# Turning seven of the sixteen Wk tiles on VectorE, and interleaving the context's second half with Wk's first tile

## The reference, cut to what matters

```python
Q = einsum('btx,dx->btd', layernorm(x), Wq) + bq
K = einsum('bpx,dx->bpd', ctx, Wk) + bk            # ctx: 4 x 64 x 2048, Wk: 2048 x 2048
attn = softmax(einsum('btd,bpd->btp', Q, K) / sqrt(2048))
x = x + tanh(g_xattn) * einsum('btp,bpd->btd', attn, ctx)
x = x + tanh(g_ffn) * ffn(layernorm(x))            # router, top-8 slots, uncertainty gate
```

## Time and profile before

| | |
|---|---|
| median of 3 runs | 1095.2 us (1094.51 to 1099.56) |
| the profiled execution | 1094.26 us |
| its span in the profile | 1092.5 us |
| TensorE busy | 1053.9 us, 96% of the span |
| VectorE, ScalarE, GpSimd busy | 70%, 51%, 17% |
| keys stage | from 0 to 137.2 us of the span |

### The profile page before, as it was taken

One profiled execution on the slowest core, in us unless ns is written; L12 is line 12 of the kernel. 1 busy time (PEld: TensorE's weight loads), 2 busy tenths in 40 slices (PEclk: granted clock), 3 DMA queues, 4 the chain that ended last, 5 costly groups with the idle time before them and its releaser, 6 DMA issues. The chain is left out here.

```text
span 1092.5 us, 19631 instructions
## 1 busy us (share of the span) xinstructions
PE 1053.9 (96%) x6890; PEld 1009.0 (92%) x6890; DVE 768.6 (70%) x1844; ACT 552.8 (51%) x860; POOL 182.7 (17%) x351
## 2 busy tenths in 40 slices
PE   6999999999998999999999999999999994999997
PEld 6999999998998999999999999999999994888886
DVE  6655546456746877777777778776877766788785
ACT  3333477654625454545454545454554543555643
POOL 0610000000002222222223131312222322000000
PEclk9999999999999999999999999999999996999999
DMA  7433646689449982744343744437353517999999
GB/s 280 145 134 135 236 175 253 265 285 280 130 144 233 233 227 79 191 134 123 107 117 113 201 124 109 121 102 212 100 142 82 149 39 226 392 389 400 404 422 382
DMA packets 106588, 218.90 MB, mean 200 GB/s; under 512 B 48052, under 2 KB 64468, under 8 KB 91608
## 3 DMA queue, kind: packets, MB, share of 16 engines
q1 hardware_dynamic: 96760, 180.68, 53.3%
q10 hardware_dynamic: 9216, 33.56, 7.9%
q0 software_dynamic: 576, 4.19, 0.9%
HBM read 174.10 MB, written 54.79 MB: 210 GB/s over the span
## 5 line engine op out<-in xcount | busy, mean ns | idle before, releaser
L56 PE MATMUL tk_bank<-b_weights,k_turned 128*128 128x384 f32 (+2 forms) x1088 | 359.4, 330 | 3.3 <-DVE k_turned L1334 1.6
L58 PE MATMUL tk_bank<-b_weights,k_turned 128*128 128x384 f32 (+2 forms) x1088 | 350.2, 322 | 0.0
L57 PE MATMUL tk_bank<-b_weights,k_turned 128*128 128x384 f32 (+2 forms) x1088 | 350.1, 322 | 0.0
L56 PEld LDWEIGHTS tk_bank<-b_weights,k_turned 128*128 128x128 f32 x1088 | 205.0, 188 | 7.4 <-issue 3.1
L57 PEld LDWEIGHTS tk_bank<-b_weights,k_turned 128*128 128x128 f32 x1088 | 205.2, 189 | 1.3
L58 PEld LDWEIGHTS tk_bank<-b_weights,k_turned 128*128 128x128 f32 x1088 | 204.6, 188 | 0.0
L1325 DVE STREAM_TRANSPOSE tk_bank<-k_rows 128x512 f32<-128x512 f32 x128 | 133.4, 1066 | 7.4 <-DMA k_rows<-in_x_dram 7.1
L1137 ACT ACTIVATE k_turned<-tk_bank 128x512 fp32r<-128x512 f32 x128 | 73.7, 595 | 82.2 <-DVE tk_bank L1325 75.1
L1334 DVE TENSOR_TENSOR k_turned<-tk_bank,k_turned 128x512 fp32r<-128x512 f32 x128 | 82.7, 685 | 8.0 <-ACT k_turned L1137 6.8
L1700 DVE TENSOR_TENSOR late_x<-late_x,ob_out 128x512 f32<-128x512 f32 x96 | 65.7, 687 | 23.9 <-PE ob_out L58 22.6
L56 PE MATMUL tk_bank<-k_turned,a_T 128*128 128x256 f32 x256 | 77.3, 302 | 0.5 <-DVE a_T L254 0.5
(11 more groups left out here) (229 smaller groups left out, 2199.8 us busy)
## 6 DMA issues: line engine op xcount, KB each, us to landing
k_rows<-in_x_dram SPq DMA_DIRECT2D x40, 1024.0 KB, 4.9
k_rows<-in_x_dram SPq DMA_DIRECT2D x128, 256.0 KB, 5.2
late_x<-in_x_dram SPq DMA_DIRECT2D x24, 1024.0 KB, 8.4
out_dram<-late_x ACTq DMA_DIRECT2D x48, 512.0 KB, 14.2
k_rows<-in_Wk_dram SPq DMA_DIRECT2D x16, 1024.0 KB, 4.8
k_rows<-in_Wq_dram SPq DMA_DIRECT2D x16, 1024.0 KB, 4.9
out_dram<-k_rows ACTq DMA_DIRECT2D x16, 512.0 KB, 11.5
b_weights<-scratch_b SPq DMA_DIRECT2D x6, 1024.0 KB, 8.0
```

The source lines that it names most:

```text
L56: pe.matmul(out, lh, rh, start=start, stop=False, skip_group_check=skip)
L57: pe.matmul(out, lh, rl, start=False, stop=False, skip_group_check=skip)
L58: return pe.matmul(out, ll, rh, start=False, stop=stop, skip_group_check=skip)
```

## The change

Tiles 2, 4, ..., 14 of Wk (seven of sixteen) are no longer transposed by TensorE. They are loaded in 32-row blocks (four DMAs of 256 KB each) into `rows[3]` and `rows[0]` by turns, and VectorE turns them with its 32x32 block transpose into the same four banks. Tile 0 and the odd tiles are still transposed by TensorE; the odd ones use `rows[1]` alone. The loop now takes two tiles at a time: in the even tile's products TensorE turns the odd tile, in the odd tile's products it turns nothing.

At the start, the groups of the context's second half alternate with those of tile 0, which go into banks 5, 6, 7, 5, and the products of tile 0 begin after the second such pair. The loads of tile 1 and of the first block tile are issued ahead of the small loads, and the DRAM copy of the context goes from the start to the end of the keys stage.

On ScalarE and VectorE: the bias is now added by ScalarE (two activations from PSUM for each tile, one for the float32 key and one for its high part), VectorE keeps the subtraction and the product with bq. The context means are row sums on ScalarE (in place, with an accumulator) instead of `bn_stats` on VectorE. Both first row sums of Wq come before the last tile's high parts. VectorE's bodies are written out in full instead of a hardware loop.

```diff
+    start_bank = [banks[i] for i in (5, 6, 7, 5)]
+    blocks_in = [m.sem("blocks_in"), rows_in[0]]
+    wk_blocks = io["Wk"].rearrange("(t k j) (q f) -> t q j k f", k=P // LANES, j=LANES, q=QUADS)
+    HALF = KC // 2
+    def key_blocks(j):
+        return rows[(3, 0)[j % 2]], blocks_in[j % 2]
+    def load_key_blocks(sp, j):
+        tile, done = key_blocks(j)
+        for q in range(QUADS):
+            sp.dma_start(tile[q * LANES:(q + 1) * LANES, :].rearrange("j (k f) -> j k f", f=QN),
+                         wk_blocks[2 * j + 2, q]).then_inc(done, 16)
...
         load(sp, 0, 0)
+        load(sp, 1, 1)
+        load_key_blocks(sp, 0)
...
-        load(sp, 1, 1)
+        sp.wait_ge(turned, C + GROUPS)
+        load_key_blocks(sp, 1)
+        for j in range(HALF - 1):
+            sp.wait_ge(turned, C + GROUPS * (j + 2))
+            load(sp, 2 * j + 3, 1)
+            if j + 2 < HALF - 1:
+                sp.wait_ge(block_turned, GROUPS * (j + 1))
+                load_key_blocks(sp, j + 2)
+            elif j + 2 == HALF - 1:
+                load_wq(sp, io, keep, 0)
+                sp.wait_ge(block_turned, GROUPS * (HALF - 2))
+                load_wq(sp, io, keep, 1)
+        sp.wait_ge(block_turned, GROUPS * (HALF - 1))
+        load_wq(sp, io, keep, 3)
+        sp.wait_ge(turned, C + GROUPS * (HALF + 1))
+        load_wq(sp, io, keep, 2)
         sp.dma_start(scr["ctx"], io["ctx"]).then_inc(keep["ctx_stored"], 16)
...
+        def turn_rows(j, g):
+            if g == 0:
+                pe.wait_ge(rows_in[1], 16 * (j + 1))
+            transpose_group(pe, bank[g], rows[1], g, ident, spread=True).then_inc(turned, 1)
+        def second_products(j):
+            for g in range(GROUPS):
+                pe.wait_ge(lo_done, C + GROUPS * (j + 1) + g + 1)
+                products(2 * j + 1, 1, g)
+        def body(j):
+            pe.wait_ge(biased, 2 * j - 1)
+            for g in range(GROUPS):
+                pe.wait_ge(block_lo, GROUPS * (j - 1) + g + 1)
+                products(2 * j, 0, g)
+                turn_rows(j, g)
+            pe.wait_ge(biased, 2 * j)
+            second_products(j)
+        def turn_start(g):
+            if g == 0:
                 pe.wait_ge(rest_in, 16)
+            pe.wait_ge(lo_done, g + 1)
+            transpose_group(pe, bank[g], crow[1], g, ident, spread=True).then_inc(turned, 1)
             if g == 0:
                 pe.wait_ge(rows_in[0], 16)
+            if g == GROUPS - 1:
+                pe.wait_ge(lo_done, GROUPS + 2)
+            transpose_group(pe, start_bank[g], rows[0], g, ident, spread=True).then_inc(turned, 1)
+        def first_products(g):
+            pe.wait_ge(lo_done, GROUPS + 2 * (g + 1))
+            products(0, 0, g)
...
+        turn_start(0)
+        turn_start(1)
+        first_products(0)
+        turn_start(2)
+        first_products(1)
+        turn_start(3)
+        first_products(2)
+        turn_rows(0, 0)
+        turn_rows(0, 1)
+        first_products(3)
+        turn_rows(0, 2)
+        turn_rows(0, 3)
         pe.wait_ge(small_in, 16 * 7)
         pe.transpose(ps_bias[:, 0:2 * KC], raw[:], ident[0:2 * KC, 0:2 * KC]).then_inc(bias_turned, 1)
...
+        second_products(0)
+        with pe.Fori(1, HALF // 2) as j:
+            body(j)
         pe.wait_ge(diag_done, 2)
...
+    def key_part(act, n, u):
+        shift = bias[:, bass.ds(n, 1)]
+        act.wait_ge(product, n + 1)
+        act.activation(kf[u][:], kp[u][:, 0:CR], ACT.Identity, bias=shift)
+        act.activation(KT[0][:, bass.ds(n, 1), :].rearrange("p o n -> p (o n)"), kp[u][:, 0:CR],
+                       ACT.Identity, bias=shift).then_inc(biased, 1)
     def low_part(dve, n, u):
+        dve.drain()
+        dve.wait_ge(biased, n + 1)
         hi = f32(KT[0][:, bass.ds(n, 1), :]).rearrange("p o n -> p (o n)")
         dve.tensor_tensor(KT[1][:, bass.ds(n, 1), :].rearrange("p o n -> p (o n)"), kf[u][:], hi,
                           ALU.subtract)
+        dve.scalar_tensor_tensor(dot[:], kf[u][:], bias[:, bass.ds(KC + n, 1)], dot[:],
+                                 ALU.mult, ALU.add).then_inc(dot_done, 1)
...
+        def body(j, first=False):
+            if not first:
+                act.wait_ge(dot_done, 2 * j - 2)
+                key_part(act, 2 * j - 1, 1)
             for g in range(GROUPS):
+                rows_hi(2 * j + 1, 1, g, j + 1)
+                if g:
+                    blocks_hi(j, g - 1)
...
+            key_part(act, 2 * j, 0)
+            blocks_hi(j, GROUPS - 1)
...
+        for r in range(2):
+            act.activation(crow[r], crow[r], ACT.Copy, accum_out=csum[:, r:r + 1]).then_inc(ctx_summed, 1)
+            body(r + 1)
...
+        key_part(act, KC - 3, 1)
+        first_sums(act)
+        for g in range(GROUPS):
+            rows_hi(KC - 1, 1, g, HALF)
+        act.wait_ge(dot_done, KC - 3)
+        key_part(act, KC - 2, 0)
...
+        def turn(j, g):
+            dve.drain()
+            tile, done = key_blocks(j)
+            if g == 0:
+                dve.wait_ge(done, blocks_count(j))
+            dve.transpose(bank[g][:].rearrange("p (c k j) -> p c k j", c=4, j=LANES),
+                          tile[:].rearrange("p (k i c) -> p c k i", k=P // LANES, c=KC)[:, 4 * g:4 * g + 4]
+                          ).then_inc(block_turned, 1)
+        def body(j, first=False):
+            if not first:
+                low_part(dve, 2 * j - 1, 1)
             for g in range(GROUPS):
+                rows_lo(j, g)
+                turn(j, g)
+                if g:
+                    blocks_lo(j, g - 1)
+            low_part(dve, 2 * j, 0)
+            blocks_lo(j, GROUPS - 1)
...
+        body(0, first=True)
+        for j in range(1, 3):
+            body(j)
...
+        body(3)
+        body(4)
         dve.wait_ge(mu_ready, 1)
         dve.tensor_copy(keep["mu_all"][:], ps_mu[:, 0:CR]).then_inc(keep["mu_done"], 1)
...
         keys["vector"](dve, first_means)
         weights_lo(0)
-        keys["vector_bias"](dve)
-        row_mean_of(1)
-        weights_lo(1)
         keys["vector_last"](dve)
+        weights_lo(1)
         row_mean_of(2)
```

More of the change, by code:

```diff
@@ L98, in keys_stage @@
     raw = mem.sb("bias_rows", [2 * KC, P])
[L99 to L100 removed]
+    csum = mem.sb("ctx_sum", [P, 2])
     diag = [mem.sb(f"diag{r}", [P, P]) for r in range(2)]
@@ L155, in tensor, with products @@
         pe.wait_ge(ident_done, 2)
[L156 to L159, removed]
-                pe.wait_ge(rest_in, 16)
[L161 to L165, removed]
+        def products(n, u, g):
+            for c in range(4 * g, 4 * g + 4):
+                ins = split_product(pe, kp[u][:, 0:CR], (T[u][0][:, c, :], T[u][1][:, c, :]),
+                                    (ctxT[0][:, c, :], ctxT[1][:, c, :]), c == 0, c == KC - 1)
+            if g == GROUPS - 1:
+                ins.then_inc(product, 1)
@@ L193, in tensor @@
-        body(0, first=True)
+        second_products(0)
+        with pe.Fori(1, HALF // 2) as j:
+            body(j)
         pe.wait_ge(diag_done, 2)
@@ L197, in tensor @@
         ins.then_inc(mu_ready, 1)
-        with pe.Fori(1, KC // 2 - 1) as j:
+        with pe.Fori(HALF // 2, HALF - 1) as j:
             body(j)
-        body(KC // 2 - 1, last=True)
+        body(HALF - 1)
     def tensor_row(pe):
@@ new lines, in scalar, with high, rows_hi, blocks_hi @@
+    def scalar(act, first_sums):
+        def high(n, u, g, count, done):
+            act.wait_ge(count[0], count[1] + g + 1)
+            act.activation(T[u][0][:, 4 * g:4 * g + 4, :], bank[g][:].rearrange("p (k n) -> p k n", k=4),
+                           ACT.Copy).then_inc(done, 1)
+        def rows_hi(n, u, g, j):
+            high(n, u, g, (turned, C + GROUPS * j), hi_done)
+        def blocks_hi(j, g):
+            high(2 * j + 2, 0, g, (block_turned, GROUPS * j), block_hi)
+        def body(j, first=False):
+            if not first:
+                act.wait_ge(dot_done, 2 * j - 2)
+                key_part(act, 2 * j - 1, 1)
+            for g in range(GROUPS):
+                rows_hi(2 * j + 1, 1, g, j + 1)
+                if g:
+                    blocks_hi(j, g - 1)
+            if first:
+                act.wait_ge(bias_turned, 1)
+                act.activation(bias[:], ps_bias[:, 0:2 * KC], ACT.Copy).then_inc(bias_kept, 1)
+                act.wait_ge(bias_kept, 1)
+            else:
+                act.wait_ge(dot_done, 2 * j - 1)
+            key_part(act, 2 * j, 0)
+            blocks_hi(j, GROUPS - 1)
+        for n, (dst, src) in enumerate(start_parts(0)):
@@ L294, in vector @@
                           keep["tgx"][:, 0:1], None, ALU.mult).then_inc(keep["mu_done"], 1)
-        with dve.Fori(1, KC // 2 - 1) as j:
+        for j in range(5, HALF - 1):
             body(j)
-        body(KC // 2 - 1, last=True)
-    def vector_bias(dve):
-        dve.wait_ge(product, KC)
-        dve.tensor_scalar(kf[1][:], kp[1][:, 0:CR], bias[:, KC - 1:KC], None, ALU.add).then_inc(biased, 1)
```

(8 more changed lines are left out.)

142 lines of the change are left out of this document (48 added, 94 removed).

## The result

The changed kernel takes 1083.15 us (median of 4 runs, 1081.90 to 1085.94) where the kernel before takes 1096.36 (4 runs, 1094.51 to 1099.56): a ratio of 0.988, with a 95% interval of 0.986 to 0.990. That is 13.2 us faster; 1080.5 with a range of 1077 to 1090 had been forecast. The profiled execution took 1081.9 us, its span is 1079.8 against 1092.5, and the mean granted clock is 0.986 in both.

The account below looks back on a forecast made before the run. TensorE was taken to bound the keys stage. From the profiled 1094.3 us, turning -13.2, start 0 and hand-over -1.3 gave 1079.8; the median was forecast at 1080.5 us, 8-in-10 range 1077 to 1090.

Parts of the forecast that it names:

- What bounds the kernel: Keys stage: TensorE, busy for all of 67.4 us, sets the pace; work taken off it ends the kernel earlier.
- Turning: Keys stage: seven tiles lose their TensorE transposes, 28 x 0.47 = 13.2 us gained; a pair of tiles takes 13.24 us.
- VectorE's load: Per pair of tiles, VectorE's transposes, copies, low parts and drains sum to 11.9 us against 13.24, 90% busy.
- The start: Context and first tiles: 0 us, the earlier start eaten by waits for tile 0 and VectorE; 1.5 better to 3 worse.
- The hand-over: Ahead of the first Wq product: early row sum and mean cut TensorE's wait from 1.54 to 0.2 us, -1.3 us.
- Moved and free: Mean's small matmuls, context copy now alongside Wq tile 4, dropped issue gaps: 0 us, worst 3 us.
- The sum: Whole kernel, profiled execution: 1094.3 - 13.2 + 0 - 1.3 = 1079.8 us; median forecast 1080.5 us.
- Rival A: Bodies 5 and 6: VectorE falls behind while GpSimd centres, block transposes held too; 1087 us, chance 0.18 including similar part losses.
- Rival B: Odd tiles' loads: the single row buffer, 7.1 us from issue to need, is the bound; slower, 1105 us, chance 0.08.
- Rival C: Keys stage: VectorE's transposes cost 1.11 us, waits and drains 0.2 more; pairs 14.6 us, no difference, 1093 us, chance 0.12.

## Why the prediction came out

**What bounds the kernel.** Right: giving TensorE its transposes back costs 12 us of the stage while VectorE's work stays.

**Turning, -13.2 us.** Right in mechanism, 1.2 too large. A pair fell to 13.23 us, forecast 13.24. The transposes were worth slightly less than 0.47 each group: with TensorE turning everything, fourteen groups take 56.47 - 30.09 = 26.38 us, 1.884 each, so a pair was 15.07 and seven pairs save 12.9. From that go two waits for VectorE that "TensorE shouldn't stop in the steady part" denied or booked elsewhere: some 0.4 to 0.7 at 30.10 (listed idle, and by starts) and 0.55 at 110.42. That leaves 11.6 to 11.9, and the run without VectorE's turning says 12.0. So the step that was off is that TensorE never stops: it does, while VectorE turns the first and the last of the seven tiles. The two starts of the run in which TensorE turns all, from its PE timeline:

```profile
30.09 0.62 PE L87 MATMUL tk_bank<-k_ident,k_rows 128*128 128x128 f32 x4
...
56.47 0.62 PE L87 MATMUL tk_bank<-k_ident,k_rows 128*128 128x128 f32 x4
```

**VectorE's load.** 11.9 us in 13.24 was 90%, drains included. The profile counts no drain as busy: 11.24 us in a pair, and with six drains of 0.10 that is 11.8. A block transpose is listed with 1.08 us, but takes 0.97 to 1.00 from its start to the next instruction's, where 1.03 was taken. The 0.10 for a drain and the 0.61 for a low part hold.

**The start, 0 us.** The waits came as laid out: tile 0 at 12 to 13 us (0.90, forecast 1), VectorE before body 1 (0.41, forecast 0.65). Body 1 began 0.5 us later than 31.15, by as much as P0 was later: 23.19 us after P0, and before it was 32.99 - 7.98 - 1.88 = 23.13. So the forecast of 0 holds. Where VectorE turns nothing, the new start does gain 0.5 us (tile 2's first group comes at 18.40 after P0, before at 18.89); in the changed kernel the wait at 30.10 eats it. The slow rate of 0.20 did not outlast the idle time at 12 us: the four transposes at 13.33 take 0.55 us in all. A step failed here that cost nothing by luck: I took the small loads to land by 20.7. The last, for `k_bu`, is issued at 12.82 and lands 10.8 us later, at 23.6, and TensorE wants it at 24.99. In four of the experiments it landed 13.0 to 13.2 us after its issue, and TensorE waited 0.62 to 0.97 for it. The PE line of one, the kernel with the transposes given back:

```profile
26.02 0.24 PE L243 MATMUL tk_bank<-k_ident,a_bias_rows 32*128 32x32 f32 x1 [0.79 <-DMA k_bu<-in_bu_dram]
```

**The hand-over, -1.3 us.** Right: the wait of 1.54 is gone entirely (0.2 was forecast), and undoing the early sums brings 1.04 back.

**Moved and free, 0 us.** Right for the changed kernel: the Wq tile issued at 125.30 landed after 9.3 us, and no Wq tile was late for TensorE. But "free" was the wrong word for the copy. Left at the start it would have cost 9.4 us in this kernel, which no step of the prediction had priced.

**The sum.** -12.0 for the turning and -2.05 for the rest make -14.06 between P0 and S, where -14.5 was forecast. The profiled execution came out at 1081.9 where 1079.8 was forecast: 0.4 of these 2.1 us belong to the working, 0.5 to P0, 0.9 to what follows S and 0.3 to what lies around the span. But for the 0.4, these are within what unchanged code scatters. The 0.4 is small because two misses cancel, which is luck: the turning gained 1.2 less than forecast, the rest 0.75 more.

**Rival A.** Its first half happened: beside GpSimd's centring a key part on VectorE is 1.4 to 1.9 us longer, and the last pair lost 0.55 us. GpSimd, and VectorE beside it, in the changed kernel:

```profile
85.77 10.42 POOL L482 TENSOR_TENSOR a_cent<-k_turned,k_mu_all 128x512 f32<-128x512 f32 x8 [84.27 <-DVE k_mu_scaled L389]
96.11 10.85 POOL L487 TENSOR_TENSOR a_cent<-a_cent,k_turned 128x512 f32<-128x512 f32 x8
```

```profile
83.54 0.42 DVE L284 TENSOR_TENSOR a_KT<-a_key_f,a_KT 128x256 fp32r<-128x256 f32 x1
83.88 0.48 DVE L286 SCALAR_TENSOR_TENSOR a_bq_dot<-a_key_f,k_bias_cols,a_bq_dot 128x256 f32<-128x256 f32 x1
...
97.71 1.27 DVE L284 TENSOR_TENSOR a_KT<-a_key_f,a_KT 128x256 fp32r<-128x256 f32 x1
98.90 1.51 DVE L286 SCALAR_TENSOR_TENSOR a_bq_dot<-a_key_f,k_bias_cols,a_bq_dot 128x256 f32<-128x256 f32 x1
...
103.98 1.08 DVE L359 STREAM_TRANSPOSE tk_bank<-k_rows 128x512 f32<-128x512 f32 x1
```

The second half, which made it 1087, did not happen: the transpose at 103.98 is as long as any. **Rival B** didn't happen, but is one transfer away. **Rival C** is refuted: 1.08 us each and drains as I had them.

## What to carry to other kernels

An operation that costs one engine twice what it costs another is still worth moving, if the dear engine is idle and the cheap one is the bound: here 0.27 us of VectorE for each 0.12 of TensorE, 12 us gained. Before calling it safe, lay out one period with both engines' lists, then look for the tightest buffer (here one row buffer, 6.9 us from free to needed), and ask which transfer could make its load late; a large copy belongs where no such load is in flight. Price a stall of TensorE of several us at more than its length, since it comes back at a lower clock: here stalls of 3.1 to 7.1 us cost 1.6 to 2.6 us on top.

## What the runs showed of the hardware

- A stop of TensorE in mid-kernel cost more than its wait. After 7.09 us idle the granted clock was 0.50 over the next 4 us and two groups took 1.9 us more than usual; after idle times of 3.11 to 5.45 us it was 0.50 to 0.57, and two groups took 1.6 to 2.6 us more.
- With a copy of 2 MB from DRAM to DRAM, itself 15.6 us in flight, a load of 1 MB issued 12 us behind it took 15.2 us; the same load without the copy took 5.5. With such a copy issued right ahead of them, five loads took 10.3 to 11.9.
- Two-input VectorE instructions on SBUF of 256 columns went from 0.42 and 0.48 us to 0.74 to 1.56 and 1.50 to 1.52 beside continuous GpSimd work; block transposes from SBUF to PSUM of 512 columns (1.06 to 1.12) did not change.
- A short wait costs TensorE more than its idle time is listed with: at 110.42 the timeline lists 0.29 us, and the pair is 0.55 longer than the others. The listed idle time counts from the listed end of a matmul, 0.28 after its start, while without a wait the next one starts after 0.12; and the first matmul behind the wait takes 0.23 to the next start.
